# Three cross attentions on Trainium2: the place of the exponentials in ScalarE's queue

## The reference

```python
q, k, v = (split_heads(q), split_heads(k), split_heads(v))
dots = jnp.einsum('bhnd,bhmd->bhnm', q, k) * scale
dots = jnp.where(mask, dots, -jnp.inf)          # the first only
attn = jax.nn.softmax(dots, axis=-1)
out = jnp.einsum('bhnm,bhmd->bhnd', attn, v)
out = out.transpose(0, 2, 1, 3).reshape(x.shape[0], x.shape[1], INNER)
return out @ Wo + bo
```

## Time and profile before

| | us |
|---|---|
| median of 3 runs | 2400.94 (2399.62 to 2401.43) |
| the profiled execution | 2401.57 |
| its span, first to last instruction | 2399.7 |
| TensorE busy | 2227.5 (93%) |
| VectorE busy | 1857.3 (77%) |
| ScalarE busy | 1493.9 (62%) |
| GpSimd busy | 686.7 (29%) |

### The profile page before, as it was taken

The page is one execution under the profiler, slowest core; times in us unless marked ns, Lnnn a source line. Parts: engine busy times, 40 slices in busy tenths (PEclk is TensorE's granted clock), DMA queues, the critical chain, the costliest instruction groups (busy, mean ns, idle before and its releaser), DMA issues.

```text
span 2399.7 us, 49297 instructions
## 1 busy us (share of the span) xinstructions
PE 2227.5 (93%) x14668; PEld 1913.3 (80%) x14669; DVE 1857.3 (77%) x4483; ACT 1493.9 (62%) x3090; POOL 686.7 (29%) x926
## 2 busy tenths in 40 slices
PE   7899999999899999995479999999998999989999
PEld 6788888888698788873257888888886788879998
DVE  3798888888876788887975887887888666866666
ACT  5566666666444677767886666666664655636666
POOL 2255555555412122210001111111102442422334
PEclk9999999999899999997589999999998999989999
DMA  8444454445201444430025445444442000114545
GB/s 216 118 141 129 142 146 142 131 138 147 69 0 37 125 132 126 138 111 16 0 67 152 135 134 152 138 145 140 140 132 62 1 1 2 38 54 141 140 140 158
DMA packets 461646, 256.58 MB, mean 107 GB/s; under 512 B 25664, under 2 KB 442332, under 8 KB 461532
## 3 DMA queue, kind: packets, MB, share of 16 engines
q1 hardware_dynamic: 461532, 255.27, 37.8%
HBM read 150.10 MB, written 105.12 MB: 106 GB/s over the span
## 4 chain that ended last, share of the span: by engine, by line
PE 75%; DVE 11%; ACT 6%; issue 5%; POOL 0%; ACTq 0%; DVEq 0%; POOLq 0%
PE ps_o L904 13%; PE ps_s L891 11%; PE ps_p L87 7%; PE ps_p L89 6%; PE ps_p L88 6%; PE ps_t L881 6%; PE ps_o L1474 3%; PE ps_t L1474 2%; PE ps_t L3129 2%; PE ps_s L3111 2%; PE ps_o L3129 2%; PE ps_s L87 2%; ACT a_keys L1022 2%; DVE a_sm L1197 2%; PE ps_s L89 2%
## 5 line engine op out<-in xcount | busy, mean ns | idle before, releaser
L904 PEld LDWEIGHTS ps_o<-a_val,a_pt 128*128 128x128 f32 (+2 forms) x3200 | 416.3, 193 | 34.9 <-issue 8.4
L904 PE MATMUL ps_o<-a_val,a_pt 128*128 128x128 f32 (+2 forms) x3200 | 426.6, 277 | 5.7 <-ACT a_pt L1059 3.6
L891 PE MATMUL ps_s<-a_keys,a_zt 128*128 128x308 f32 (+1 forms) x1024 | 414.3, 491 | 14.6 <-ACT a_keys L1022 9.8
L1031 ACT ACTIVATE a_stage<-ps_p 128x512 f32<-128x512 f32 (+1 forms) x370 | 221.2, 598 | 277.0 <-PE ps_p L89 275.5
L1197 DVE TENSOR_REDUCE a_sm<-a_e 128x16 f32<-128x1232 f32 (+1 forms) x192 | 234.3, 1220 | 179.4 <-ACT a_e L1067 178.9
L1059 ACT ACTIVATE a_pt<-ps_t 128x512 f32<-128x512 f32 (+1 forms) x448 | 225.1, 505 | 144.0 <-PE ps_t L881 142.7
L1022 ACT ACTIVATE a_keys<-ps_p 128x308 f32<-128x308 f32 x603 | 256.8, 427 | 79.5 <-PE ps_p L89 79.0
L87 PE MATMUL ps_p<-ct_hi,a_mt_hi 96*128 (+1 forms) x603 | 292.2, 485 | 0.0
L881 PE MATMUL ps_t<-ident,a_e 128*128 128x128 f32 (+1 forms) x1600 | 261.8, 276 | 25.1 <-POOL a_e L1214 13.6
L1067 ACT ACTIVATE a_e<-a_e 128x1232 f32<-128x1232 f32 (+1 forms) x192 | 203.9, 1062 | 52.8 <-DVE a_e L1189 36.4
L1214 POOL TENSOR_TENSOR a_e<-a_e,a_rs 128x539 f32<-128x539 f32 (+1 forms) x192 | 165.8, 891 | 231.3 <-DVE a_rs L1202 230.0
(11 more groups left out here) (437 smaller groups left out, 4939.4 us busy)
## 6 DMA issues: line engine op xcount, KB each, us to landing
a_vals<-a_stage SPq DMA_DIRECT2D x160, 512.0 KB, 3.5
a_val<-a_vals SPq DMA_DIRECT2D x128, 576.0 KB
f_w<-in_L_ffn_W_dram SPq DMA_DIRECT2D x129, 256.0 KB, 2.6
a_vals<-a_stage SPq DMA_DIRECT2D x40, 416.0 KB
a_val<-a_vals SPq DMA_DIRECT2D x64, 256.0 KB
a_val<-a_vals SPq DMA_DIRECT2D x128, 40.0 KB
x<-in_x_dram SPq DMA_DIRECT2D x8, 512.0 KB, 7.0
out_dram<-x SPq DMA_DIRECT2D x7, 512.0 KB, 6.7
```

The lines of the kernel that those rows point to most:

```text
L891: eng.matmul(c.ps_s[:, b, 0:nh * KEYS], zt, keys[:, h0:h0 + nh, :], start=True, stop=True)\
L904: mm = eng.matmul(c.ps_o[:, (i % 2) * P:(i % 2 + 1) * P], self.pt[0:r, n, :], self.val[0:r, i % 2, n, :], start=(n == 0), stop=(n == self. ...
L1031: eng.activation(self.stage[0:n, slot, BANK * (v % 2):BANK * (v % 2) + BANK], bank[0:n, :], ACT.Copy)\
```

## The change

With 16 heads ScalarE issues the exponentials of batch t+1 ahead of the copies of the turned probabilities of batch t, as it does already with 8 heads, in all batches but t = 0. With 8 heads the order in t = 0 changes the other way. The first window is now written out for ScalarE in all three attentions, and the loop runs over windows 1 to 6. The core of the diff:

```diff
-                if more and H == 8:
+                early = not (isinstance(w, int) and t == 0)
+                if more and early:
                     self.exponentials(eng, t + 1, (k + 1) % 2)
...
                 for j in range(self.uses):
                     self.copy_chunks(eng, j, self.pt, self.t_use(w, i, j, last), self.t_slot(i, j, last))
                     if j < self.uses - 1:
                         copy_next(1)
-                if more and H > 8:
+                if more and not early:
                     self.exponentials(eng, t + 1, (k + 1) % 2)
-                copy_next(self.NB)
+                copy_next(self.NB, 1)
...
-        first = 0
-        if self.left:
-            window(0, False)
-            first = 1
-        with eng.Fori(first, self.WINDOWS - 1) as w:
+        window(0, False)
+        with eng.Fori(1, self.WINDOWS - 1) as w:
             window(w, False)
         window(self.WINDOWS - 1, True)
```

More of the change, by code:

```diff
@@ new lines, in count_keys, with key_number, keys_for @@
+    @staticmethod
+    def count_keys(plan):
+        return sum(kind == "k" for mine in plan for kind, _, _ in mine)
+    def key_number(self, w, place, last=False):
+        plan = self.tail if last else self.plan
+        before = sum(kind == "k" and p < place for mine in plan for kind, _, p in mine)
+        return self.first - self.vuses + 2 * self.heads * w + before
+    def keys_for(self, w, par, b, last):
+        if not self.ahead:
+            head = sum(self.head_span(b)) - 1
+            for i in range(3) if par == 0 else range(3, 7):
+                for kind, h, place in self.plan_of(i, last):
+                    if kind == "k" and h == head:
+                        return self.key_number(w, place, last)
+            return self.key_number(w - 1, next(place for kind, h, place in self.plan[-1] if kind == "k" and h == head))
+        order = [h for k in range(GT) for h in self.freed_by(k, 1 - par)]
+        h0, nh = self.head_span(b)
+        return self.heads + 2 * self.heads * w + self.heads * par + max(map(order.index, range(h0, h0 + nh)))
@@ L731, in key_group @@
     def key_group(self, i):
-        return 1 + (i + 1) // GT
+        return 1 + (i + (2 if self.ahead else 1)) // GT
     def keys_use(self, w, par, b, last):
         head = sum(self.head_span(b)) - 1
+        if self.ahead:
+            i = GT * par + head // self.quads - 2
+            mine = self.plan_of(i, last) if i >= 0 else self.plan[i]
+            return self.use(w if i >= 0 else w - 1, next(place for kind, h, place in mine if kind == "k" and h == head))
         for i in range(3) if par == 0 else range(3, 7):
@@ L883, in turn_chunks, with scores @@
         mm.then_inc(self.t_done.sem, 1)
[L885 removed]
+    def scores(self, eng, t, b, par, k, first=False):
         c = self.core
@@ L958, in tensor @@
         eng.wait_ge(self.before.sem, self.before.at(1))
-        for u in range(self.first):
+        for u in range(self.lead):
             if u >= 5:
                 eng.wait_ge(self.proj_copied.sem, self.proj_copied.at(u - 4))
+                if self.split and u - 5 >= self.vuses:
+                    eng.wait_ge(self.key_split.sem, self.key_split.at(u - 5 - self.vuses + 1))
             if u < self.vuses:
@@ L1282, in body @@
                     self.shift(eng, t + 2, k % 2, found)
+                if self.split and k == 1 and not last:
+                    u = 1 + self.gcyc * g + 2 * self.uses
+                    self.split_zt(eng, g + 1, 1 - par, u, (1 + self.gcyc * par + 2 * self.uses) % 2)
                 self.residual(eng, t, k)
@@ L1323, in gpsimd @@
         self.copy_window(eng, 1)
-        if self.next_stats and not self.setup:
+        if self.next_stats and not self.setup and not self.split:
             self.after.split_weights(eng)
```

241 lines of the change are left out of this document (206 added, 35 removed).

## The result

| | before | after |
|---|---|---|
| median, us | 2400.28 (2395.02 to 2401.43, 4 runs) | 2454.62 (2448.5 to 2456.09, 4 runs) |
| the profiled execution | 2401.57 | 2456.09 |
| its span | 2399.7 | 2454.2 |

The changed kernel takes 1.0208 times as long, 95% interval 1.0193 to 1.0224: slower by 54 us at the medians, 54.5 at the spans of the two profiled executions.

A forecast was written before the change was run, and what follows sets the result against it. TensorE, without gaps in the steady parts, was taken as the bound. a2 12.6 + 6.8 + 1, a0 17.5 + 6.8 + 1 and clock 3 gave 48.7 us on 2401.6: 2450 us, range 2428 to 2478.

The forecast's parts named there:

- The deciding step: a2: exponentials start (E) 0.26 us after turns start (T), delaying the first copy; third group of turns loses 0.30 us.
- a2, steady: Third attention (16 heads), seven windows: six stalls of 0.30 us in eight batches, 1.8 us a window, 12.6 us in all.
- a0, steady: First attention (16 heads, mask): stalls 0.9 at window place i = 7, 1.4 at i = 0; 2.5 us a window, 17.5 in all.
- The last windows: Last windows of a0 and a2: four loops each 2.3 us longer, less the lead: 6.8 us each, 13.6 in all.
- lead: End of a0's and a2's last windows: the exponentials' earlier start, 2.4 us, is used up and comes off the loss.
- clock: Last windows: TensorE gaps of 2 to 4 us lower its clock; at most 10 us, taken as 3.
- The rest: Starts of a0 and a2 cost 1 us each; written-out code costs nothing; a1 0.1 us or nothing.
- Faster: Rival: exponentials fit ahead of the turns' start, copies are not late, a0's 1.3 us a window are won: 2392; chance 0.06.
- Only the ends pay: Rival: no stall in the steady parts, only last windows, clock and starts cost: 2420, from 2410 to 2436; chance 0.13.
- The clock falls in the steady parts: Rival: TensorE's clock at 0.88 over 112 batches, 125 us more, 2575 us; chance 0.02.
- More: Rival: stalls of 0.40 us, 4.0 us a window in a0, clock at its bound: 2475 us; chance 0.13.

The follow-up runs named there:

- the first experiment: Changed kernel, but with 16 heads the exponentials stand behind the first copy of turned probabilities and the projection copy after it: 2395.49 us, ratio 0.9962.
- the halves: Changed kernel with 16-head exponentials in two instructions, heads 0 to 7 ahead of the first copy, 8 to 15 behind it: 2441.86 us, ratio 1.015.
- the kernel with repeated turns: Changed kernel with the second group of turns done seven times in four last-window batches of a0 and a2: 2447.7 us profiled; a second execution 5739.5.
- written out alone: Changed kernel with the old order everywhere with 16 heads, leaving only ScalarE's written-out first window: 2405.77 us, ratio 1.0002.
- the kernel without maxima ahead: Changed kernel, but with 16 heads VectorE no longer takes the first bank's maxima ahead of the sum in the last window: 2432.42 us, ratio 1.0122.
- the old order at the ends: Changed kernel, but in the last window of a0 and a2 the exponentials stand behind the copies as before: 2434.27 us, ratio 1.0122.

## Why the prediction was right, and where it was not

**The deciding step** held to hundredths: E = T + 0.25 for 0.26, first copy T + 1.37 for 1.38, third group T + 2.01 for 2.03. That this delay, and not something else in the change, is the steady loss is shown by the first experiment, which leaves the exponentials 1.2 us earlier than they were and frees the copy (a2's window back at 71.64), and by the halves, which in a2 take away the stall wherever E doesn't wait for VectorE.

**a2, steady**: 12.6 us and 1 for the start were forecast, 12.9 measured. A window loses 2.08 us for 1.8. From one batch's T to the next, six of the eight batches are longer by 0.27 to 0.38 us and two by 0 and 0.06 (means of five windows): the stalls are where they were forecast, and each is about 0.34 instead of 0.30. The third group starts 0.28 later (T + 2.01 for T + 1.73), and the two turns of a woken group take 0.44 us where those of the earlier trace rows take 0.38. Seven such windows would be 14.6 us. Between the additions they lose 12.9, because the seventh window of them loses only 0.5. The addition that ends it is where VectorE's lead shows:

```profile
1787.83 0.60 PE L881 MATMUL ps_t<-ident,a_e 128*128 128x128 f32 x4
...
1797.86 0.28 DVE L1221 TENSOR_TENSOR x<-ps_o,x 128x128 f32<-128x128 f32 x1
```
```profile
1830.65 0.60 PE L988 MATMUL ps_t<-ident,a_e 128*128 128x128 f32 x4
...
1838.81 0.28 DVE L1370 TENSOR_TENSOR x<-ps_o,x 128x128 f32<-128x128 f32 x1
...
1846.64 1.24 ACT L1208 ACTIVATE a_e<-a_e 128x1232 f32<-128x1232 f32 x1 [1.94 <-DVE a_e L1338]
```

The first two rows are of the kernel before. T of the last window's first batch and the addition that belongs to it lie 10.03 us apart before and 8.16 after. From T to T, first batch to 57th, a2 loses 15.7 us: the 14.6 and 1.1 more at the start.

**a0, steady**: 17.5 forecast, 17.4 measured. The two long stalls are there; exponentials and turns at i = 7 and i = 0, of the changed kernel:

```profile
444.73 0.60 PE L988 MATMUL ps_t<-ident,a_e 128*128 128x128 f32 x4
...
445.62 1.23 ACT L1208 ACTIVATE a_e<-a_e 128x1232 f32<-128x1232 f32 x1 [2.84 <-DVE a_e L1314]
```
```profile
454.10 0.60 PE L988 MATMUL ps_t<-ident,a_e 128*128 128x128 f32 x4
...
455.32 1.23 ACT L1208 ACTIVATE a_e<-a_e 128x1232 f32<-128x1232 f32 x1 [1.05 <-DVE a_e L1314]
```

E is 0.89 and 1.22 us behind T, and the third group starts 0.92 and 1.28 us later than before, for forecast stalls of 0.9 and 1.4. The window is longer by 2.69 for 2.5; seven of them are 18.8, and from T to T the 56 batches lose 19.2. That the additions show 17.4 is in part luck: here too the addition of the 57th batch follows its T sooner, by 9.18 us for 10.92.

**The last windows** lose 24.2 us between the additions, where 13.6 and 3 for the clock were forecast. Counted from T of the 57th batch they lose 20.6 (9.0 in a0, 11.6 in a2), and the steady parts have the other 3.6. The parts:

| | predicted | measured |
|---|---|---|
| four longer loops in a0 and a2, at full clock | 18.4 | about 17.9 (9.3 in a2, 8.6 in a0) |
| the lead that comes off at the end | -4.8 | -3.6 (1.9 in a2, 1.7 in a0); between the additions it falls into the stretches of 56 batches |
| the clock | 3 | about 8 |
| the end behind a0's loops | 0 | -1.4 |

The split goes by the kernel with repeated turns: its loops and its end stand for full clock (a2: 9.3 us more than before in four loops, and the same 8.6 us from the last exponentials to the last addition; a0, in the same way, 8.6 more and 1.4 less), and what the changed kernel needs over that is the clock's, 4.2 us in a2 and 3.6 in a0. For the first of the four loops, where the repeated turns are themselves in the way, I took the changed kernel's (9.21 and 9.71). The 1.4 less is not the lead: with the old order in a0's last window the same end took 12.1 us in one kernel and 13.9 in another.

The **lead** held as a step and was over-sized by 1.2 us. It cannot be seen between the additions and the exponentials, for both follow VectorE: the exponentials of 1846.64 come 7.83 us behind the 57th addition, and those of the kernel before (1805.69) just as far. Against T it can: the exponentials issued in the last window's first batch of a2 start at T + 0.08 (before T + 2.62), and those of 1846.64, issued two batches on, are 16.0 us behind that batch's T where they were 17.9. So 1.9 of 2.5 us were still in hand when the four long loops began, and by the 60th batch both kernels have E at T + 2.39.

The **clock** is the term that was mis-sized. It was priced with the turn and the scores at half clock and then cut from the bound of 10 to 3, for no reason in a row; about 8 were measured. The first long loop of each attention kept the full clock (1.00; 9.21 us in a2). In the three loops behind it and in the batch that ends the attention the clock was down each time (0.83 or 0.84 over each of the loops), and each of the eight took 0.7 to 1.2 us longer than with the gap filled. The bound held, the value inside it did not. In the steady parts the clock stayed at 1.00, with 36 waits of 0.36 us in a2. Read as a rule, what the Trainium skill tells of another kernel (TensorE: Matmul & The Clock Gate, "A second HAM failure mode: psum-queue depth-cycling") would have the clock go up and down there; the rows do not bear it out for idle times of that length. For a wait of 3 us in every round of the last windows they show a lower clock; for a single one they do not, since in the kernel with repeated turns the batch behind a2's loops waits 3.07 us at full clock.

**The rest.** Starts: 2 us forecast, 0.3 in a0 and 1.1 in a2 seen from T to T; the first batch of a2 takes 10.7 or 12.2 us in kernels of the old order there (before; written out alone), so one trace cannot tell 1 us from nothing. That the written-out window costs nothing is shown by the kernel with that alone. a1 came out 1.9 us longer, but this is not the change: with a1's new order in batch 0 it takes 297.8 (the kernel without maxima ahead) or 300.1 (changed), with its old one 298.1 (before; the old order at the ends) or 300.1 (written out alone). What makes the two levels is open. Between a0 and a1 the changed kernel takes 2.2 us less than the one before; in the other kernels that stretch takes 144.1 to 147.8, with the loop written out alone 147.8, so this is not shown to be the change either.

**The rivals.** "Faster" would have needed E ahead of T; it is T + 0.25. "Only the ends pay" fell with the third group at T + 2.01. "The clock falls in the steady parts" fell at 1.00. "More" was the nearest: the clock came 5 us nearer to its bound, and the stalls of a2 were 0.34. The total came within 5 us of 2450 with some luck: from T to T the steady parts with their starts lose 34.9 us for 32.1, the clock 5 more and the lead 1.2 less than forecast, and against that stand 0.5 in the loops, 1.4 at the end of a0 and 0.9 in the stretches between, which the prediction had not.

Not tried: giving the third group of turns a bank of its own, which would take the dependence away. All eight banks that the kernel declares are in use (three for ps_s, two each for ps_p and ps_t, one for ps_o), so it would have to be taken from another step.

## To carry to other kernels

Before an instruction is moved forward in an in-order queue, find the instruction behind it for which the bounding engine waits, and measure from start to start how much later that one may come; here the slack was 0.44 us and the instruction took 1.12. An idle time of an engine that isn't the bound is no gain to be had, however long its column is (89.4 us of VectorE's were worth nothing in a2), and here the right place was behind the urgent short instruction rather than ahead of it. Price loops at the end of a stage apart, with the order of every engine in them and at the clock that their own gaps bring about, since a few batches there can lose as much as fifty in the steady part. And where stretches are cut by one engine's instructions, that engine's own lead is lost from view: cut them by the bounding engine as well.

## What the runs showed of the hardware

- TensorE's granted clock was 1.00 with waits of 0.3 to 0.4 us once in a batch of 9 us, and 0.84 over two loops of the last window with one wait of 3.07 us in each 10.3 us; with the gap filled by repeated turns it was 1.00 again, and the loop 1.0 us shorter. One wait of 3.07 us right behind those filled loops left it at 1.00, and so did the first long loop of the changed kernel.
- VectorE's subtraction of three banks of a_e took 1.57 us by itself and 3.57 beside GpSimd's copies of the text; and 1.57 again when these were made to wait. That the two engines get in each other's way is also what the Trainium skill says (GPSIMD Engine Reference, section 1, Specifications: the SBUF interfaces are shared with VectorE, with contention where a VectorE instruction has two SBUF inputs, as this subtraction has). The trace agrees, 3.57 us for 1.57; here it made ScalarE wait 1.3 us in each window of a0, and the window was 1.1 us shorter without it.
